# Unpadded stacks and 32-row score tiles in a causal attention, and weights rounded by GpSimd, in a two-layer transformer kernel

## The reference

```python
# layer 0: attention, 16 heads of 8, causal
qkv = einsum('btd,ed->bte', x, Wqkv)            # split into q, k, v of [b, h, t, 8]
scores = clip(einsum('bhtd,bhsd->bhts', q, k) * 8**-0.5, -10, 10) + causal_mask
o = softmax(scores) @ v;  x = layernorm(x + o @ Wout.T)
# layer 0: experts, top 2 of 8, F = 256
h = silu(x @ W1[e].T) * (x @ W2[e].T);  x = layernorm(x + sum_e gate_e * (h @ W3[e].T))
# layer 1: attention, 16 heads of 8, full, rotary embedding on q and k over all 128 columns
o = softmax(q @ k.T * 8**-0.5) @ v;  x = layernorm(x + o @ w_out.T + b_out)
# layer 1: router with a hidden layer, experts top 2 of 4, H = 512
h = gelu(xi @ We1[e] + be1[e]);  x = layernorm(x + sum_e w_e * (h @ We2[e] + be2[e]))
```

## Time and profile before

| what | us |
| --- | --- |
| timed runs, median (lowest to highest) | 1720.16 (1710.94 to 1721.71) |
| profiled execution, own time | 1729.45 |
| its span, first to last instruction | 1727.2 |
| TensorE busy in the span | 1566.1 |
| VectorE busy | 1410.2 |
| ScalarE busy | 1167.6 |
| GpSimd busy | 108.6 |
| exponentials of the causal attention, L487, 192 of them | 265.7 |
| clips L517, 272 of them | 163.5 |
| causal score products L443, 768 of them | 143.0 |
| causal value products L459, 1536 of them | 157.6 |
| maxima of the full attention, L816, 512 of them | 588.3 |

### The profile page before, as it was taken

How to read it: one execution, slowest core, us unless ns; L and a number is a source line. 1 busy time by engine, 2 the same in 40 slices (tenths; PEclk the granted TensorE clock), 3 DMA queues, 4 the chain that set the end, 5 groups by cost and what they waited for, 6 DMA issues and landing times.

```text
span 1727.2 us, 32148 instructions
## 1 busy us (share of the span) xinstructions
PE 1566.1 (91%) x11104; PEld 801.1 (46%) x11104; DVE 1410.2 (82%) x2503; ACT 1167.6 (68%) x1779; POOL 108.6 (6%) x187
## 2 busy tenths in 40 slices
PE   6899999969999999968999999999999978888887
PEld 3433333346656655633333333333333336666665
DVE  3688999867777777777999999999999827887777
ACT  3798999833333333215999999999999966655565
POOL 2000000000100111020000000000000000010000
PEclk9898999989999999975999999999999989999999
DMA  7482222222322221240111111111111010000100
GB/s 214 146 234 85 91 91 92 69 69 63 100 100 91 71 83 62 91 154 3 44 38 48 54 37 38 37 43 37 42 54 43 18 39 14 20 21 26 34 7 13
DMA packets 68461, 112.97 MB, mean 65 GB/s; under 512 B 23088, under 2 KB 32176, under 8 KB 67712
## 3 DMA queue, kind: packets, MB, share of 16 engines
q1 hardware_dynamic: 68352, 111.48, 20.6%
HBM read 67.79 MB, written 43.65 MB: 65 GB/s over the span
## 4 chain that ended last, share of the span: by engine, by line
PE 57%; DVE 19%; issue 9%; ACT 6%; DMA 4%; SPq 3%; POOL 1%; ACTq 0%; DVEq 0%; POOLq 0%
PE full_o L731 14%; PE max_pair L702 11%; PE causal_o L459 6%; PE hid_pair L1028 6%; PE triple L443 6%; PE score L716 3%; DVE negmax_h L816 3%; PE bank L1119 2%; DVE hid L1435 2%; DVE lin_u L1431 2%; ACT cprobs L487 1%; PE bank L1131 1%; DMA k_scr<-qk_hi 1%; DVE st L1263 1%; PE hid_pair L960 1%
## 5 line engine op out<-in xcount | busy, mean ns | idle before, releaser
L816 DVE TENSOR_REDUCE negmax_h<-max_pair 128x2 f32<-128x1024 f32 x512 | 588.3, 1217 | 23.4 <-PE max_pair L702 23.3
L782 ACT ACTIVATE probs<-score 128x512 f32<-128x512 f32 x1024 | 547.2, 596 | 78.6 <-PE score L716 59.2
L731 PE MATMUL full_o<-probs,v_st 128*32 128x256 f32 x4096 | 330.8, 395 | 17.7 <-ACT o_sb L790 17.7
L716 PE MATMUL score<-q_st,k_st 32*128 32x512 f32 x1024 | 316.6, 503 | 0.8 <-ACT probs L782 0.7
L487 ACT ACTIVATE cprobs<-triple 128x1536 f32<-128x1536 f32 x192 | 265.7, 1454 | 22.6 <-PE triple L443 19.9
L702 PE MATMUL max_pair<-k_st,q_st 32*128 32x512 f32 x1024 | 264.2, 515 | 10.9 <-DVE negmax_h L816 9.6
L1225 ACT ACTIVATE act_s<-hid_pair 128x512 f32<-128x512 f32 x128 | 76.5, 597 | 192.6 <-PE hid_pair L1028 192.5
L702 PEld LDWEIGHTS max_pair<-k_st,q_st 32*128 32x128 f32 x1024 | 97.6, 188 | 234.4 <-DVE negmax_h L816 179.9
L1028 PE MATMUL hid_pair<-x_hi,w_hi 128*128 128x512 f32 x384 | 198.8, 518 | 6.8 <-ACT act_s L1230 6.8
L517 DVE TENSOR_SCALAR cprobs<-cprobs 128x1536 f32<-128x1536 f32 (+6 forms) x272 | 163.5, 625 | 0.4 <-ACT cprobs L487 0.4
L459 PE MATMUL causal_o<-cprobs,v_st 128*32 128x512 f32 (+3 forms) x1536 | 157.6, 507 | 3.2 <-DVE cprobs L517 3.2
(11 more groups left out here) (139 smaller groups left out, 1631.4 us busy)
## 6 DMA issues: line engine op xcount, KB each, us to landing
o_scr<-o_sb SPq DMA_DIRECT2D x64, 256.0 KB, 2.1
gate_all<-gate_scr SPq DMA_DIRECT2D x32, 512.0 KB, 5.6
k_st<-k_scr SPq DMA_DIRECT2D x64, 128.0 KB, 2.8
q_st<-q_scr SPq DMA_DIRECT2D x128, 64.0 KB, 2.4
q_st<-q_scr SPq DMA_DIRECT2D x16, 512.0 KB
k_st<-k_scr SPq DMA_DIRECT2D x64, 104.0 KB
q_scr<-qk_hi SPq DMA_DIRECT2D x24, 256.0 KB, 4.1
k_scr<-qk_hi SPq DMA_DIRECT2D x24, 256.0 KB, 4.2
```

What stands on the lines that cost most here:

```text
L716: nc.tensor.matmul(sbank[L.score_bank(e)][:, :], k_st[p][rows, j, kt * P:(kt + 1) * P], q_st[p][rows, q0:q0 + w], start=True, stop=True, t ...
L731: last = nc.tensor.matmul(full_o[SLOT * j:SLOT * (j + 1), cols], v_st[p][:, kt, j, :], probs[s % NP][:, j, cols], start=(kt == 0 and part ...
L782: nc.scalar.activation(probs[s % NP][:, L.HEADS[j], :], sbank[L.score_bank(e)][:, :], ACT.Exp, scale=SCALE).then_inc(L.exp_done, 1)
L816: nc.vector.tensor_reduce(negmax_h[:, qt // TPC, half, heads[0]:heads[1] + 1:2, qt % TPC], ring[slot][:, :, :], AXX, ALU.max, negate=True) ...
```

## The change

- The causal scores run on tiles of 32 rows, one head each. Both stacks are [128, 1024], without zeroes, and are shared by both attentions in a place of their own, outside the overlays; `w_hi` and `w_lo` have such places too, and `w_raw` moves into the attention's overlay.
- "Twins" are made of the two chunks of one head instead of two heads of one chunk and stand behind the first key block of the second chunk; the output of chunk 0 is copied after slot 7 instead of 5. A round has 27 clip instructions instead of 28 and as many columns, and the last slot has two blocks of values instead of three.
- No clearing of the stacks, no pad stores, no padded scratch. When the last causal scores are done GpSimd sets both key stacks to one; the loads for the full attention are 24 rows for each head, keys and queries apart (eight DMAs a round), so that rows 24 and 25 keep the ones. The loads of rounds 0 and 1 move into the loop over the first experts' chunks.
- The small weights are loaded after the stacks of round 5, the raw weights after those of round 6, the rotary tables after those of round 8; the raw weights of layer 1 in the first round of the full attention.
- GpSimd rounds: four instructions a layer on 128x2048 (a copy and a subtraction for each of two weights), one at a time after the staging of values, in causal rounds 10 to 13 and full rounds 2 to 5. The instructions of ScalarE and VectorE for it go; both wait for the result at the start of the expert stage.
- The value stacks of layer 1 are filled by GpSimd instead of VectorE. Loops of SP and GpSimd are written out.

```diff
+        twins = [("twins", [(qc, qc * TPC + 2, j, 2 * P * qc, 2 * P) for qc in range(CPB)]) for j in self.HEADS]
...
+                if kt == 0:
+                    pieces += twins
...
-            pieces += [("twins", [(qc, d + 2, j, 0, 2 * P), (qc, d + 2, j + 1, 2 * P, 2 * P)]) for j in (0, 2)]
...
-            for bk, j, kt, q0, w, off in L.order_of(n):
-                r, rows = rows_of(j)
-                last = nc.tensor.matmul(triple[n % 2][:, bk, off:off + w], k_st[p][rows, j, kt * P:(kt + 1) * P],
+                r, rows = slot_rows(j, SLOT)
+                last = nc.tensor.matmul(triple[n % 2][:, bk, off:off + w], k_st[p][rows, kt * P:(kt + 1) * P],
...
+        def pool_round_weights(layer, k, lower):
+            if lower:
+                nc.gpsimd.tensor_tensor(w_lo[k][:, :], w_raw[k][:, :], w_hi[k][:, :].bitcast(F32),
+                                        ALU.subtract).then_inc(w_lower, 1)
+            else:
+                nc.gpsimd.tensor_copy(w_hi[k][:, :], w_raw[k][:, :]).then_inc(w_upper, 1)
...
         def pool_causal(pool, L):
-            for p in range(2):
-                nc.gpsimd.memset(k_st[p][:, :, :].bitcast(F32), 0.0).then_inc(L.zeroed, 1)
-            nc.gpsimd.memset(pad_rows[:, :], 0.0).then_inc(pads_set, 1)
...
+            for i in range(NG - 2):
+                pool.wait_ge(L.pv_done, L.values_before(i + 1))
+                pool_stage_v(pool, L, i + 2, i % 2)
+                if 0 <= i - WEIGHTS_FROM < 4:
+                    pool_weights(pool, 0, i - WEIGHTS_FROM)
+            pool.wait_ge(L.scores_ready, L.N * NG)
+            for p in range(2):
+                nc.gpsimd.memset(k_st[p][:, :].bitcast(F32), 1.0).then_inc(layers[1].ones_set, 1)
...
-            sp_store_pads(sp)
...
+            for i in range(4, NG - 2):
+                next_round(i, i % 2)
+                if i == 5:
+                    for t, name in WEIGHTS:
...
+                if i == 6:
+                    for k, name in enumerate(("w1", "w2")):
...
+                if i == 8:
+                    sp.dma_start(rope_a[:, :], d["rope_a"]).then_inc(rope_loaded, 16)
...
             sp_keep_o(sp, L, 0, 0)
+            sp.dma_start(w_raw[0][:, :], d["we1"]).then_inc(raw_loaded[0], 16)
+            sp.dma_start(w_raw[1][:, :], d["we2"].rearrange("p n c -> p (n c)")).then_inc(raw_loaded[1], 16)
             sp_load_aug(sp, L, 1, 1, 0)
...
         def act_end(act, st, layer):
+            act.wait_ge(w_lower, 2 * (layer + 1))
             for n in range(SPC):
                 act_beside(act, st, n, None, 0, 0, layer)
-                if n == plan[layer].o_turn:
-
-                    for k in range(2):
-                        act.wait_ge(raw_loaded[k], 16 * (layer + 1))
-                        act.wait_ge(layers[layer].o_saved, CPB * NG)
-                        nc.scalar.activation(w_hi[k][:, :], w_raw[k][:, :], ACT.Copy).then_inc(w_upper, 1)
...
-                dve_fill_values(dve, layers[1])
...
-                    pool_clear_full(pool, layers[1])
+                    pool_fill_values(pool, layers[1])
...
-                    sp_first_full(sp, layers[1])
...
+                if c in (2, 3):
+                    sp.wait_ge(layers[1].ones_set, 2)
+                    sp_load_full(sp, layers[1], c - 2, c - 2)
```

More of the change, by code:

```diff
@@ L43 @@
 LATE = (0, 2)
-ROWS = 2 * SLOT
+HALVES = 3 * DK
 SUMS = H * CH // P
@@ L67, in __init__ @@
         assert len(pieces) == 3 * self.N and self.N % 2 == 0 and self.N % CP == 0
-        self.last_kt = [qc * TPC + 2 for qc in range(CPB)]
+        self.last_kt = [2, KT - 1]
         self.where, ends = {}, {}
@@ L79, in __init__ @@
         self.V = len(ends)
-        self.first_chunk = sum(b[0] == 0 for b in ends)
+        order = [b for blocks in self.blocks_at for b in blocks]
+        self.first_chunk = order.index((0, self.last_kt[0])) + 1
+        assert order[-1] == (1, self.last_kt[1])
+        assert all(b[0] > 0 for b in order[self.first_chunk:])
         self.clips = []
@@ L273, in build_program @@
         g_halves = sb("g_halves", [P, TPC, 2 * E0])
+        k_st = [sb(f"k_st{p}", [P, T], F32R) for p in range(2)]
+        q_st = [sb(f"q_st{p}", [P, T], F32R) for p in range(2)]
+        w_hi = [sb(f"w_hi{k}", [P, NH * P], F32R) for k in range(2)]
+        w_lo = [sb(f"w_lo{k}", [P, NH * P], F32R) for k in range(2)]
         with ExitStack() as overlay:
@@ L298, in build_program @@
             ot = osb("ot", [P, CH])
-            gate_all = [osb("gate_all0", [P, 2, CH])]
-            gate_bc = [gate_all[0][:, i, :] for i in range(2)]
+            res = [osb("res0", [P, TPC, D])]
+            xs = [osb("xs0", [P, TPC, D])]
+            with ExitStack() as layer_only:
+                gate_rows = layer_only.enter_context(nc.sbuf_tensor("gate_rows", [E0, CH], F32))
+            gate_t = osb("gate_t", [2 * E0, CH], F32R)
             act_s = [osb(f"act_s{i}", [P, CH]) for i in range(2)]
@@ L305, in build_program @@
             hid = [osb(f"hid{i}", [P, CH]) for i in range(2)]
+            gate_all = [osb("gate_all0", [P, 2, CH])]
+            gate_bc = [gate_all[0][:, i, :] for i in range(2)]
             y_sb = osb("y_sb", [P, CH])
[L307 to L312, removed]
+            res.append(osb("res1", [P, TPC, D]))
+            xs.append(osb("xs1", [P, TPC, D]))
             expert_raw = osb("expert_raw", [2 * E0, E0, P])
@@ L700, in pe_pair @@
             for k, j in enumerate(heads):
-                r, rows = slot_rows(j)
+                r, rows = slot_rows(j, HALVES)
                 last = nc.tensor.matmul(ring[slot][:, k, :], q_st[p][rows, qt * P:(qt + 1) * P],
-                                        k_st[p][rows, j, half * CH:(half + 1) * CH], start=True, stop=True,
+                                        k_st[p][rows, half * CH:(half + 1) * CH], start=True, stop=True,
                                         tile_position=(r, 0))
@@ L889, in pool_full @@
             pool_cut(pool, L, 0, 0)
-            with pool.Fori(0, NG // 2 - 1) as u:
-                for p in range(2):
-                    pool_cut(pool, L, 2 * u + p, 1)
-                    pool_cut(pool, L, 2 * u + p + 1, 0)
-                    pool.wait_ge(L.pv_done, L.values_before(2 * u + p + 1))
-                    pool_stage_v(pool, L, 2 * u + p + 2, p)
+            for i in range(NG - 2):
+                pool_cut(pool, L, i, 1)
+                pool_cut(pool, L, i + 1, 0)
+                pool.wait_ge(L.pv_done, L.values_before(i + 1))
+                pool_stage_v(pool, L, i + 2, i % 2)
+                if 0 <= i - 2 < 4:
+                    pool_weights(pool, 1, i - 2)
             pool_cut(pool, L, NG - 2, 1)
@@ L1457, in dve_end @@
                 dve_front[0].link(nc.vector.memset(sc8[:, :, E1:8], -1.0))
+            dve.wait_ge(w_lower, 2 * (layer + 1))
             for n in range(SPC):
                 dve_beside(dve, st, n, None, 0, 0, layer)
[L1460 to L1465 removed]
             if layer == 0:
```

110 lines of the change are left out of this document (35 added, 75 removed).

## The result

The changed kernel takes 1996.64 us (median; 1989.98 to 1999.85) against 1720.93 (1710.94 to 1722.03): a ratio of 1.1607, 95% interval 1.1559 to 1.1655. That is slower by 16%, where 1706 and at most 1724 were forecast. The products of the full attention changed too, which neither the list nor the diff above shows: the products for the maxima ("pairs") read 24 rows of a tile (`HALVES`) and the scores 26, where both read 32.

A forecast was written before the change was run, and what follows sets the result against it. TensorE was taken as the bound, ScalarE and VectorE nearly level. Terms summed to −14.1, taking the profiled 1729.45 to 1715.4, or 1706 as a timed median (1700 to 1712); with rivals 1690 to 1724, E outside.

The forecast's parts named there:

- Part 6: Second attention: 24-row loads free; +1.5 for half clock lasting longer in the first attention, +1 for a reload behind raw weights.
- Rival E: Causal rounds: less busy TensorE gets the lower clock, 3.6 per fall; one every round gives 1764; chance 0.09.
- Part 1: Causal scores on 32-row tiles: 0.43 for 0.66 a slot, ScalarE becomes the bound at 16.1 a round; −18.
- rival B: Causal rounds: VectorE becomes the bound at 16.8 and every shut-out counts in full, 1721; chance 0.18.
- D: Causal scores: 32-row products don't run side by side, no gain from tiles, 1724; chance 0.06.
- Part 2: Pads and weights out of early causal rounds: the stall between rounds 3 and 4 goes, −7; new places cost +0.5.
- rival C: Later causal round: its load stalls behind the weights as round 4's did, 1712; chance 0.08.
- Part 3: GpSimd rounding in causal rounds 10 to 13 shuts VectorE out; overruns 0.7 per copy, 3.3 per subtraction, two each: +8.
- Rival A: Shut-out of VectorE by GpSimd is free, swallowed by VectorE's slack and TensorE's new room: 1696; chance 0.18.
- Parts 4 and 5: End of causal attention and transition to feed-forward: GpSimd clears +1.7 and −0.2; earlier router copy, fewer value blocks −1.6.
- Part 7: Last transition: the subtractions removed there stood beside the router, far ahead of its end; 0 (−4.5 if not covered).

The follow-up runs named there:

- e1: Changed kernel with pairs and scores of the full attention on 32 rows again, queries padded with zeroes: 1707.58 against 1727.51, ratio 0.9895.
- e2: Kernel before, with pairs of the full attention on 24 rows and scores on 26 instead of 32: 2014.28, before 1727.51.
- e9: Changed kernel with 32 rows in full rounds 0 and 1 alone, 24 and 26 rows after: 1708.56 against 1719.14, ratio 0.9938.
- e6: Kernel before, with pairs on 24 and scores on 26 rows in full rounds 4 to 7 alone: 1718.15, before 1720.26.
- e12: e9's kernel with a TensorE pause in full round 8, waiting for six GpSimd clears: 1868.24.
- e13: e1's kernel with a TensorE pause in full round 8, waiting for six GpSimd clears: 1728.14, before 1729.30.
- e7: Kernel before, with only the causal scores on 32-row tiles, new order of pieces and turn of the copy: 1708.66 against 1720.26, ratio 0.9925.
- e10: e1's kernel with GpSimd's rounding in smaller instructions, one every half round in causal rounds 9 to 14: 1697.04 against 1719.14, ratio 0.9861.
- e4: Kernel before, with scores of the full attention on 26 rows, pairs on 32: 1753.02, before 1727.51.
- e5: Kernel before, with pairs of the full attention on 26 rows, scores on 32: 1786.71, before 1720.26.
- e3: Kernel before, with pairs of the full attention on 24 rows, scores on 32: 2021.14, before 1727.51.

## Why the prediction was wrong

**The step that failed** is in Part 6: "Loads shrink to 24 rows; the first two move into the feed-forward stage, where SP has pauses: nothing." It priced the loads and not the products that read them, on 24 and 26 rows. They cost 288 us, through the clock, which they keep at 0.50. The row that could have warned was used: TensorE at 0.50 for 17.5 us while busy throughout. I read it as a delay of fixed length and carried it to the causal attention as +1.5; it was a stage whose recovery the change touched. e1, e2 and e9 show the cause from three sides, and e6, e12 and e13 show its form: it is the rise that the short products prevent. Why the chip grants the lower clock to products with fewer rows no run shows.

**Rival E** had the sign and the kind, with a chance of 0.09, but the place wrong (causal rounds) and the price too (3.6 a round, against 18.5). Its argument went by TensorE's busy share, 86 against 88%; the stage that stayed at 0.50 is busy 99%. The Trainium skill, page "TensorE: Matmul & The Clock Gate", Part 1, says that the throttled state is the default and that activity releases it; here a stage that the profile counts as busy for 902.79 of 910.00 us did not release it, and the measurement decides.

**Part 1** held: 0.42 a slot for 0.43, rounds of 16.12 for 17.27, 1.15 × 16 = 18.4 for 18. ScalarE is the bound, as it is busy 120.00 of 120.00, so rival B (VectorE the bound) and D (no overlap) fell.

**Part 2** held: rounds 3 and 4 were 20.77 and 20.91, 7.1 above two steady ones, and are 16.12 and 16.11. No load stalled at the new places (0 for +0.5), so rival C fell. e7 keeps the pause with Part 1 alone.

**Part 3** was mis-sized: rounds 11 to 14 took 18.40, 21.66, 16.56 and 21.56, 13.7 above four of 16.12, for a forecast of 8. GpSimd's instruction waits for the values of rounds 10 to 13 and so falls into the round after each. GpSimd's and VectorE's timelines after:

```profile
237.90 1.90 POOL L578 CAST w_hi<-w_raw 128x2048 fp32r<-128x2048 f32 x1
...
256.15 4.54 POOL L575 TENSOR_TENSOR w_lo<-w_raw,w_hi 128x2048 fp32r<-128x2048 f32 x1
...
238.23 2.11 DVE L516 SCALAR_TENSOR_TENSOR cprobs<-cprobs,bound 128x512 f32<-128x512 f32 x1
...
256.38 4.86 DVE L516 SCALAR_TENSOR_TENSOR cprobs<-cprobs,bound 128x512 f32<-128x512 f32 x1
```

The estimated 1.94 and 4.5 were 1.90 and 4.54, and the clip lasts as long as the subtraction beside it. TensorE then stands idle 3.52 us (the row at 261.96 above) for a forecast overrun of 3.3. What the sum lacked comes after that: the values behind the idle time take 1.94 instead of 1.07, as the clock falls (0.71 in the window 262 to 273), and the round loses 5.5 instead of 3.5. Behind the first copy the clock fell in this run too (0.53 from 241.0 to 244.6), and its round lost 2.3; in e1, where it stayed at 1.00 there, it lost 0.7, as forecast. e10 agrees with the model by stretches: parts that fit the slack cost 1.0 in all. Rival A, a free shut-out, fell for the long instructions.

**Parts 4 and 5**: from the end of the last causal exponential to the first of the full attention 448.0 became 446.2, −1.8 for a forecast of −0.1. In e2 to e6, whose code there is that of the kernel before, the same stretch takes 445.2 to 449.9, so neither figure can be told from nothing. The copy itself did move. The router's result is now copied right behind it:

```profile
340.04 1.87 PE L1089 MATMUL bank<-wg,xt 128*128 128x8 f32 x8 [0.77 <-ACT xt L1183]
...
341.95 0.19 DVE L1271 COPY sc<-bank 128x32 f32<-128x32 f32 x1 [0.75 <-PE bank L1089]
```

It starts 0.04 after the router's end, where it was 1.19. **Part 6's** other terms: causal round 0 is 3.4 above a steady one (before 2.8), +0.6 for +1.5, and no more than noise, as that round alone takes 19.67 to 23.07 in six traces of the old causal part and 17.47 to 19.56 in six of the new one. The reload of round 1 costs nothing in e1, whose round 1 takes 37.90, and GpSimd's rounding costs nothing beside the maxima there: its four instructions of 1.90 and 4.55 stand in rounds 3 to 6, of 37.96 to 37.97, and the maxima beside them last 1.22 to 1.23 for 1.22 on average. **Part 7** held: −0.4 to the end.

With the rows restored (e1) the ratio is 0.9895; the forecast was 1706/1720.16 = 0.992, inside e1's interval and e9's. So the sum without that step agrees with the measurement, and the step itself is 288 us where it said nothing. How near the trace comes up to the full attention (−16.8 for −15.1) is in part luck. The causal attention gains 11.5 us where Parts 1, 2 and 3 and the +1.5 of Part 6 make it 15.0, as GpSimd's rounding costs more. Most of the rest is that the first causal exponential came 3.5 earlier (52.0 for 55.6), and traces with one and the same start differ by as much (51.8 to 55.6 in the kernel before and e2 to e6).

## What to carry to other kernels

Don't take an edit that makes a matrix product smaller in rows for free because the columns stay: ask what it does to the granted clock of its stage, above all where that stage is entered at half clock. A row that shows a busy TensorE at half clock for a while can be a warning that the stage barely recovers; look at which products run there, and keep them full until the clock is up. A long GpSimd instruction beside a busy VectorE cost here what it exceeded the slack by; cut it into parts that fit the slack and spread them, and add the clock's fall to a TensorE pause that remains.

## What the runs showed of the hardware

- The granted clock has a memory. With the same 24- and 26-row products in the loop it stood at 0.50 for the whole stage (the changed kernel, and e2) or at 1.00 for 573 us (e9), by what ran in the first rounds; a pause of 6.5 us changed it from the second to the first (e12).
- Rows of zeroes count: e1 and e2 differ from their base by rows that add nothing to the result, and by 289 and 287 us.
- After the stage's first exponential the clock rose within 11 (e6) to 44 us (e7) with 32 rows, after 121 with 26-row scores (e4), after 205 with 26-row pairs (e5), and not in 900 us with 24-row pairs (e3). e4 and e5 are single runs.
- GpSimd's work needn't cost what it lasts: a stretch with GpSimd busy 16.92 us in pieces lost 1.0, the same stretch with 14.50 us in long instructions 11.5 (e10, e1).
